# Graph network kernel, message pass: gates behind gelus, update gelu out of PSUM, half of the second normalisation on ScalarE, tick order changed; start terms loaded three batches ahead

## The reference, cut to what matters

```
h = relu(layernorm(x)); x = x + attention(h)           # layer 0
h = relu(layernorm(x)); x = x + layer1(h)              # layer 1, the "message pass"
h = relu(layernorm(x)); x = x + propagate(h)           # layer 2, 16 rounds
h = relu(layernorm(x)); x = x + gcn(h)                 # layer 3

# layer 1
edge_input = concat(h[src], edge_attr)                 # 96 + 32 features
messages   = gelu(edge_input @ mW1 + mb1) @ mW2 + mb2
gates      = sigmoid(gelu(edge_input @ gW1 + gb1) @ gW2 + gb2)
aggregated = segment_sum(messages * gates, dst)
update     = gelu(concat(h, aggregated) @ uW1 + ub1) @ uW2 + ub2
y          = h + update
layer1     = (y - mean) * rsqrt(var + 1e-5) * ln_g + ln_b
```

## Time and profile before

| | |
|---|---|
| median of 3 runs | 11957.47 us (11951.58 to 11964.21) |
| profiled execution | 11956.96 us |
| its span | 11955.2 us |
| PE busy | 6883.6 us, 58% |
| DVE busy | 6471.5 us, 54% |
| ACT busy | 4318.2 us, 36% |
| POOL busy | 8488.0 us, 71% |
| mean granted TensorE clock | 0.738 of 2.4 GHz |

### The profile page before, as it was taken

The page is one execution under the profiler, slowest core; times in us unless marked ns, Lnnn a source line. Parts: engine busy times, 40 slices in busy tenths (PEclk is TensorE's granted clock), DMA queues, the critical chain, the costliest instruction groups (busy, mean ns, idle before and its releaser), DMA issues. The chain is left out here.

```text
span 11955.2 us, 140496 instructions
## 1 busy us (share of the span) xinstructions
PE 6883.6 (58%) x20977; PEld 4313.5 (36%) x20977; DVE 6471.5 (54%) x24207; ACT 4318.2 (36%) x14541; POOL 8488.0 (71%) x8647
## 2 busy tenths in 40 slices
PE   4687677975655556556565565555556555672000
PEld 4566566664433323323333332333323323352000
DVE  6577896898844444444444444444444444575444
ACT  5698566877722222222222222222222222373000
POOL 6675765536777777777777777777777777776777
PEclk7665667877777777777777777777777777896555
DMA  7998885668854444444444444444444444473221
GB/s 246 304 251 239 267 276 150 188 182 271 259 152 140 118 115 116 114 114 117 113 118 114 114 116 114 118 113 114 118 114 117 113 115 118 150 233 123 64 66 55
DMA packets 1059890, 1804.54 MB, mean 151 GB/s; under 512 B 515278, under 2 KB 525948, under 8 KB 1059661
## 3 DMA queue, kind: packets, MB, share of 16 engines
q1 hardware_dynamic: 777325, 1384.14, 34.9%
q0 software_dynamic: 282336, 418.19, 16.1%
HBM read 1070.12 MB, written 738.89 MB: 151 GB/s over the span
## 5 line engine op out<-in xcount | busy, mean ns | idle before, releaser
L351 POOL DMA_INDIRECT r_g<-y_t,idx_s x5768 | 5545.6, 961 | 1984.6 <-issue 1856.9
L1895 DVE SCALAR_TENSOR_TENSOR F<-r_g,scan_s,F 128x96 f32<-128x96 f32 x5488 | 1769.4, 322 | 3981.9 <-DMA r_g<-y_t,idx_s 3088.0
L1995 PE MATMUL r_pu<-r_S,ident 128*128 128x384 f32 x2688 | 1734.2, 792 | 2803.7 <-DVE r_S L1897 2803.7
L2023 ACT ACTIVATE H<-r_pu,kc_e 128x96 f32 (+1 forms) x5474 | 1340.3, 355 | 5542.5 <-PE r_pu L1995 5508.8
L1995 PEld LDWEIGHTS r_pu<-r_S,ident 128*128 128x128 f32 x2688 | 678.5, 278 | 3553.5 <-DVE r_S L1897 3219.8
L1897 DVE SCALAR_TENSOR_TENSOR r_S<-r_S,scan_s,r_g 128x96 f32<-128x96 f32 x5488 | 1716.3, 313 | 0.0
L1977 PE MATMUL r_pu<-H,ident 128*128 (+2 forms) x2744 | 1530.5, 649 | 93.4 <-DMA r_c<-c_t 87.8
L1978 PE MATMUL r_pu<-r_c,ident 128*128 128x384 f32 (+1 forms) x2744 | 1347.3, 579 | 0.0
L1977 PEld LDWEIGHTS r_pu<-H,ident 128*128 128x128 f32 x2744 | 776.4, 284 | 766.8 <-issue 656.9
L1978 PEld LDWEIGHTS r_pu<-r_c,ident 128*128 128x128 f32 x2744 | 666.8, 243 | 560.9 <-issue 361.9
L2282 PE MATMUL e_pc<-e_S,B 128*128 128x96 f32 x2 | 0.7, 474 | 1050.9 <-DVE e_o L2326 1050.9
(11 more groups left out here) (329 smaller groups left out, 12095.3 us busy)
## 6 DMA issues: line engine op xcount, KB each, us to landing
r_c<-c_t SPq DMA_DIRECT2D x686, 384.0 KB
y_t<-H SPq DMA_DIRECT2D x672, 384.0 KB
r_g<-y_t,idx_s POOLq DMA_INDIRECT x5880, 2.5
kv_t<-n_kv SPq DMA_DIRECT2D x49, 776.0 KB, 6.7
y_t<-d_yx SPq DMA_DIRECT2D x98, 384.0 KB
agg_t<-e_S SPq DMA_DIRECT2D x49, 416.0 KB, 4.5
x1s_t<-e_xb SPq DMA_DIRECT2D x50, 384.0 KB, 4.9
h_t<-e_h SPq DMA_DIRECT2D x50, 384.0 KB, 5.3
```

What stands on the lines that cost most here:

```text
L351: G.indirect_dma_start(out=to(j), out_offset=None, in_=table, in_offset=bass.IndirectOffsetOnAxis(ap=idx_s[:, h, j:j + 1], axis=0)).then_i ...
L1895: own.add(V.scalar_tensor_tensor(out=F[:, 0:D], in0=g[:, j, :], scalar=scan_s[:, h, j, 1:2], in1=F[:, 0:D], op0=ALU.mult, op1=ALU.add))
L1995: last = T.matmul(pu[h % 2][g][:], ident[:], S[:, h % 2, 4 * g:4 * g + 4, :], start=False, stop=True)
L2023: last = A.activation(v[:, j, :], pu[h % 2][j // 4][:, j % 4, :], ACT.Copy, scale=k[:, j, 0:1])
```

## The change

In the message pass:

- The update's gelu is no longer applied in SBUF. TensorE turns the hidden values as they are, and ScalarE's copy out of PSUM becomes the gelu.
- Of the second normalisation, columns 4 to 7 stay on VectorE (`scale2`, in two operations over 384 elements). Columns 0 to 3 are done on ScalarE (`norm2`, four Relu activations with scale and bias); VectorE prepares their bias by one small product. SyncE's store waits for both.
- Both tanh of a tick stand together, first in ScalarE's tick, then both roots, then all gelus.
- The order in a tick and some lags change on all engines but GpSimd.

In the rounds c has four tiles instead of two and is loaded three batches ahead instead of one, and so is H in the first round. To make room, some tiles (`dst_i`, most weights) are freed before the rounds.

```diff
-        def gelu(b, n, h):
-            after(act, s_pr, b + 1)
-            A.activation(ur[:, h % 2], ur[:, h % 2], ACT.Gelu).then_inc(s_gr, 1)
...
-                A.copy(uT[0:D, h % 2, g, :], pu[0:D, :]).then_inc(s_ut, 1)
+                A.activation(uT[0:D, h % 2, g, :], pu[0:D, :], ACT.Gelu).then_inc(s_ut, 1)
...
+        def norm2(b, n, h):                                    # ScalarE
+            act.wait_ge(s_st[h], 32 * n)
+            after(act, s_rn2, b + 1)
+            for j in range(HALF):
+                last = A.activation(yx[:, h, j, 0:D], yx[:, h, j, D:2 * D], ACT.Relu,
+                                    scale=rn2[:, h, 0, j:j + 1], bias=rn2[:, h, 1, j:j + 1])
+            last.then_inc(s_yn, 1)
...
-        def norm2(b, n, h):                                    # VectorE
+        def scale2(b, n, h):
             own6.step(b)
             after(dve, s_mv2, b + 1)
             dve.wait_ge(s_st[h], 32 * n)
-            own6.add(V.tensor_tensor(yx[:, h, :, 0:D], yx[:, h, :, D:2 * D],
-                                     mv2[:, h, :, 0:1].to_broadcast([P, J, D]), ALU.subtract))
+            after(dve, s_yn, b - 3)
+            v = yx[:, h, HALF:J, 0:D]
+            own6.add(V.tensor_tensor(v, yx[:, h, HALF:J, D:2 * D],
+                                     mv2[:, h, HALF:J, 0:1].to_broadcast([P, J - HALF, D]), ALU.subtract))
...
+            V.scalar_tensor_tensor(out=rn2[:, h, 1, 0:HALF], in0=mv2[:, h, 0:HALF, 0], scalar=-1.0,
+                                   in1=rn2[:, h, 0, 0:HALF], op0=ALU.mult, op1=ALU.mult).then_inc(s_rn2, 1)
...
         def store(b, n, h):                                    # SyncE
             after(sp, s_y0, b + 1)
+            after(sp, s_yn, b + 1)
...
-        skewed(sp, (6, load_u), (16, store), (0, edges_only(load)), (9, load_h1), (11, load_xb),
-               (7, edges_only(store_sums)), total=NX)
+        skewed(sp, (6, load_u), (14, store), (0, edges_only(load)), (9, load_h1), (10, load_xb),
+               (8, edges_only(store_sums)), total=NX)
...
-        skewed(pe, (3, hidden_m(0)), (7, turn_gelu(0)), (3, hidden_g(0)), (3, hidden_m(1)),
-               (3, hidden_g(1)), (4, edges_only(message(1))), (2, edges_only(turn(0))),
-               (4, edges_only(message(0))), (2, edges_only(turn(1))), (8, outer_layer(1)),
-               (7, turn_gelu(1)), (8, outer_layer(0)), (6, edges_only(carry)), total=NX)
+        skewed(pe, (8, outer_layer(0)), (3, hidden_g(0)), (7, turn_hidden(0)), (3, hidden_m(0)),
+               (8, outer_layer(1)), (4, edges_only(message(1))), (3, hidden_g(1)),
+               (2, edges_only(turn(0))), (7, turn_hidden(1)), (3, hidden_m(1)), (2, edges_only(turn(1))),
+               (4, edges_only(message(0))), (6, edges_only(carry)), total=NX)
...
-        skewed(dve, (10, scale), (11, update), (6, hidden), (9, add(1)), (9, add(0)), (9, stats),
-               (5, gated(1)), (12, norm2), (5, gated(0)), (11, stats2), (5, total), total=NX)
+        skewed(dve, (7, hidden), (9, add(0)), (10, scale), (12, scale2), (6, total), (11, stats2),
+               (9, add(1)), (9, stats), (10, update), (5, gated(1)), (5, gated(0)), total=NX)
...
# the rounds
-                            after(sp, s_up, r * NB + b - 1)
+                            after(sp, s_up, r * NB + b - 3)
                             sp.sem_inc(s_turn_s)
-                            sp.dma_start(cs[:, h % 2], slots_of(c_t, 0, b)).then_inc(s_c[h % 2], 16)
+                            sp.dma_start(cs[:, h], slots_of(c_t, 0, b)).then_inc(s_c[h], 16)
...
-                        skewed(sp, (1, store), (-1, load))
+                        skewed(sp, (1, store), (-3, load))
```

More of the change, by code:

```diff
@@ L17 @@
 K = 4
+HALF = J // 2
 OF = [len(range(h, NB, K)) for h in range(K)]
@@ L273, in program, with weight @@
         weight_loads = []
-        def weight(name, parts, width, rows=D + 1):
-            t = sb(name, [rows, width])
+        def weight(name, parts, width, rows=D + 1, ctx=None):
+            t = sb(name, [rows, width], ctx=ctx or nodes)
             for r0, r1, c0, c1, a in parts:
@@ L285, in col @@
             return v.rearrange("(n a) -> n a", a=1)
+        w_3 = weight("w_3", [(0, D, 0, D, W3)], D, D, outer)
+        r_rows = weight("r_rows", [(0, 1, 0, D, row(ln_g)), (0, 1, D, 2 * D, row(ln_b)),
+                                   (0, 1, 2 * D, 3 * D, row(b3))], 3 * D, 1, outer)
+        r_all = sb("r_all", [P, 3, D])
+        nodes = outer.enter_context(ExitStack())
+        dst_i = sb("dst_i", [P, CH], I32, nodes)
         w_kvq = weight("w_kvq", [(0, D, 0, D, Wk), (0, D, D, 2 * D, Wv), (0, D, 2 * D, 3 * D, Wq),
@@ L301, in program @@
         c_u1 = weight("c_u1", [(0, D, 0, 1, col(ub1))], 1, D)
[L302 to L306, removed]
+        w_mu = sb("w_mu", [D + 1, D], F32, nodes)
         iroot = sb("iroot", [P, CHS], F32, nodes)
@@ L1409, in carry, with turn_hidden @@
                             T.matmul(pm[:, 0:D], B[:], S[:, h, J - 1, :], start=True, stop=True).then_inc(s_cr, 1)
-                    def turn_gelu(g):
+                    def turn_hidden(g):
                         def run(b, n, h):
-                            after(pe, s_gr, b + 1)
+                            after(pe, s_pr, b + 1)
                             after(pe, s_ut, 2 * b + g)
@@ L1492, in norm @@
                         ln_norm(act, b, hs[:, h % 2], ln[:, h % 2], rn[:, h], s_rn, ACT.Identity).then_inc(s_ln, 1)
[L1494 to L1497, removed]
+                    def norm2(b, n, h):
[5 more added lines that the diff above has]
+                        last.then_inc(s_yn, 1)
+                    skewed(act, (5, tanh(1)), (5, tanh(0)),
                            (11, lambda b, n, h: ln_root(act, b, mv2[:, h], rn2[:, h], s_mv2, s_sd2)),
-                           (7, gelu_turned(1)), (2, edges_only(turned(1))), total=NX)
+                           (9, lambda b, n, h: ln_root(act, b, mv[:, h], rn[:, h], s_mv, s_sd)), (3, gelu_g(0)),
+                           (7, gelu_u(0)), (3, gelu_m(0)), (9, norm), (2, edges_only(turned(0))), (3, gelu_g(1)),
+                           (-2, edges_only(slots)), (7, gelu_u(1)), (4, edges_only(masks)), (3, gelu_m(1)),
+                           (2, edges_only(turned(1))), (12, norm2), total=NX)
                 @block.vector
@@ L1598, in norm2 @@
                         own6.end()
-                        V.scalar_tensor_tensor(out=yx[:, h, :, 0:D], in0=yx[:, h, :, 0:D], scalar=0.0,
-                                               in1=rn2[:, h, 0, :].unsqueeze(2).to_broadcast([P, J, D]),
+                        V.scalar_tensor_tensor(out=rn2[:, h, 1, 0:HALF], in0=mv2[:, h, 0:HALF, 0], scalar=-1.0,
+                                               in1=rn2[:, h, 0, 0:HALF], op0=ALU.mult, op1=ALU.mult).then_inc(s_rn2, 1)
+                        V.scalar_tensor_tensor(out=v, in0=v, scalar=0.0,
+                                               in1=rn2[:, h, 0, HALF:J].unsqueeze(2).to_broadcast([P, J - HALF, D]),
                                                op0=ALU.max, op1=ALU.mult).then_inc(s_y0, 1)
-                    skewed(dve, (10, scale), (11, update), (6, hidden), (9, add(1)), (9, add(0)), (9, stats),
-                           (5, gated(1)), (12, norm2), (5, gated(0)), (11, stats2), (5, total), total=NX)
+                    skewed(dve, (7, hidden), (9, add(0)), (10, scale), (12, scale2), (6, total), (11, stats2),
+                           (9, add(1)), (9, stats), (10, update), (5, gated(1)), (5, gated(0)), total=NX)
                     dve.wait_ge(s_y0, NX)
+                    dve.wait_ge(s_yn, NX)
                     first.add(V.tensor_copy(zx[:, 0:2 * D], yx[:, NB % K, 0, :]))
@@ L1977, in start @@
                                 T.matmul(to, ident[:], cols(H, b)[:, c, :], start=True, stop=False)
-                                T.matmul(to, ident[:], cs[:, h % 2, c, :], start=False, stop=False)
+                                T.matmul(to, ident[:], cs[:, h, c, :], start=False, stop=False)
                         def add(b, n, h):
```

17 lines of the change are left out of this document (8 added, 9 removed).

## The result

The changed kernel takes 12013.34 us (median of 5 runs, 11999.72 to 12015.95), the kernel before beside it 11952.9 (5 runs, 11936.65 to 11964.21): ratio 1.0052, interval [1.0040, 1.0064]. It is slower by some 60 us. Forecast: 11997, range 11930 to 12060. The profiled execution has a span of 12011.3 us, against 11955.2: +56.1.

A forecast was written before the change was run, and what follows sets the result against it. VectorE was taken to pace the message pass at 15.0 us a tick, gathers the rounds; a new ring through SyncE's store gives 35 x 1.4 = 49 us, other ticks -9, rounds zero: 11957 + 40 = 11997 us, range 11930 to 12060.

The forecast's parts named there:

- The ring: Message pass: ScalarE's norm to Relus, SyncE's store to h1 load, landing, VectorE, closing once per tick; 11.8 us plus landing.
- The landing: Message pass, h1 load behind two 384 KB stores: 4.6 us from issue to landing, where the median was 3.5.
- The tick: Message pass: 16.4 us a tick in the changed kernel, ends 14.9 and 18.1, against 15.0 before.
- SyncE's part: Message pass, SyncE's queue: two stores, then edge load to h1 load, 3.3 us of the ring.
- rival 1: Message pass: the ring closes but the h1 load's landing stays 3.5 us; tick 15.3, +1 us, 11958; chance 0.20.
- Rival 4: Message pass: h1 load runs only when stores are through, landing 5.2, tick 17.0, +61 us, 12018; chance 0.13.
- full ring ticks: Message pass, ticks 14 to 48, where stores and edge loads both run: 35 ticks x 1.4 us = 49 us.
- The light ticks: Message pass, ten full ticks beside the ring's (9 to 13, 49 to 53): -9 us.
- Rival 2: Message pass: the ring has unseen slack, VectorE stays the bound; tick 13.8, -54 us, 11903; chance 0.13.
- The split of the second norm: Message pass, VectorE: two operations halved to 384 elements, one small product added; net -0.6 us a tick.
- The rounds: Fourteen middle rounds: start-term loads three batches ahead change nothing, since gathers pace a round at 502.6 us; zero.
- Rival 3: Message pass: TensorE's clock falls to 0.62, its work of 17.9 us becomes the tick; +93 us, 12050; chance 0.12.

The follow-up runs named there:

- f3: Changed kernel with the message pass's store moved in SyncE's tick from ahead of the edge load to behind the h1 and xb loads: 11888.37 us, 0.9954 of before.
- g4: Changed kernel with ScalarE's four Relus moved from its tick's end to right ahead of the first norm, SyncE's order kept: 11926.0 us, 0.9949 of before.
- g3: Changed kernel with the second norm wholly on VectorE again, so the store waits for VectorE alone: 11956.11 us, 0.9975 of before.
- g1: Changed kernel with two rows of the second norm on ScalarE instead of four (HALF = 2): 12016.38 us, 1.0023 of before.
- g2: Changed kernel with SyncE's edge load moved behind the h1 and xb loads, the store still ahead of them: 11992.42 us, 1.0005 of before.
- f1: The changed kernel again, no edit: 12011.34 us beside 11944.65 for the kernel before, 1.0056.
- f2: The kernel before again, no edit, one profiled run: 11968.16 us.
- f4: Kernel before with only the rounds' part of the change (four start-term tiles loaded three batches ahead, SBUF moves): 11942.97 us, 1.0001 of before.

## Why the prediction was right, and where it wasn't

**The mechanism: right.** The ring ScalarE, SyncE, landing, VectorE was forecast with its links in order; the turn of 16.65 us has these and no other. It was cut or shortened at five places, and the tick fell each time: at SyncE's order (f3), at ScalarE's order (g4), at the wait (g3), at its Relus (g1), at the edge load (g2). The landing changed only along with g2, and VectorE's 0.96 us was not touched.

**The tick: right by luck, since two errors cancel.** Forecast 16.4, measured 16.65 in that turn. ScalarE 7.2 against 7.1, VectorE 0.95 against 0.96. SyncE's part was forecast as 3.3 and is 4.9: I took the edge load's issue from a tick in which no stores stood ahead of it; right behind two stores of 384 KB its second transfer takes 1.56 us to issue (1.35 in the tick before), and its third 0.7. The landing was forecast as 4.6 and is 3.3 with its hand-over (median 3.6), as rival 1 had it. When the load gets out at 2324.15, the DMA engines' rate has fallen to 145 GB/s in that microsecond, from 286 and 244 in the two before, so the stores are mostly through. Rival 4 (5.2, strictly behind the stores) is wrong here. In g2, where the load goes out 1.39 us behind the first store, the rival's way of counting (the stores hold the engines for 5 us) gives 3.5 + 3.6 = 7.1, and the median is 5.1, so about half of it holds.

**The cost of the full ring ticks: nearly right.** By the norms, here of the kernel before,

```profile
2031.66 2.62 ACT L340 ACTIVATE e_ln<-e_h,e_rn 128x96 f32<-128x96 f32 x7
...
2573.39 2.97 ACT L340 ACTIVATE e_ln<-e_h,e_rn 128x96 f32<-128x96 f32 x8
```

the 4th to the 40th batch; in the changed kernel the 4th and the 39th:

```profile
2009.46 2.97 ACT L341 ACTIVATE e_ln<-e_h,e_rn 128x96 f32<-128x96 f32 x8 [1.11 <-DVE e_rn L334]
...
2595.13 2.97 ACT L341 ACTIVATE e_ln<-e_h,e_rn 128x96 f32<-128x96 f32 x8 [4.46 <-DVE e_rn L334]
```

35 ticks take 585.7 us, 16.7 each; before, 36 ticks took 541.7, 15.05 each (the first 35 of them 529.0, 15.1 each). The 35 ticks cost 585.7 - 529.0 = 57 us, where I had 35 x 1.4 = 49. The trace of f1 repeats the 585.7 (585.8), and two more traces of the kernel before's message pass (f2, f4) have 529.8 and 527.0.

**The light ticks: wrong in sign at the end.** I counted -9 us for the ticks without a full ring. The pass does begin sooner: add(0) or add(1) first runs at 1961.7, 10.6 us before the 1972.26 of the earlier trace rows. But the ring goes on when the edge loads have ended, since the stores still run: the h1 load then goes out 1.14 us behind the store, the add follows 6.0 us or more behind it, and the norms still start every 15.3 to 15.8 us for four ticks. And the last batch has a new wait that the prediction did not list:

```profile
2706.94 0.40 SPq L1344 DMA_DIRECT2D agg_t<-e_S  x1
```

```profile
2713.00 0.94 POOL L1370 DMA_INDIRECT Z<-agg_t,idx_f  x1 [120.02 <-DMA agg_t<-e_S]
```

```profile
2715.52 0.26 DVE L1547 TENSOR_TENSOR e_S<-Z,e_pm 128x96 f32<-128x96 f32 x1 [15.35 <-DMA Z<-agg_t,idx_f]
```

These are timelines of SyncE, GpSimd and VectorE. The last store of the sums goes out at 2706.94, GpSimd's single gather Z waits for it, and VectorE waits 15.35 us for the gather. The last row of the last batch's sums had started at 2689.3:

```profile
L1534 DVE SCALAR_TENSOR_TENSOR e_S<-e_S,scan_s,e_g x392: 308/319/385, 1928.3 to 2689.3; 128x96 f32<-128x96 f32 x196
```

Before, the last such row starts at 2642.9 and the store follows at 2643.3:

```profile
L1342 SPq DMA_DIRECT2D agg_t<-e_S x49: 343/361/623, 1937.0 to 2643.3; - x49
```

The store of the sums stands behind the x2s store in SyncE's tick, so it too waits for ScalarE's Relus. I followed the h1 load behind the blocked store and not the sums store behind both. The Relus are not all of it: in g3, whose store doesn't wait for ScalarE, VectorE still waits 5.19 us for this gather, and in g4, whose Relus are early, 10.60. The change also moved the sums store one tick later (lag 8, not 7), and no run has that apart.

```profile
2622.53 0.26 DVE L1538 TENSOR_TENSOR e_S<-Z,e_pm 128x96 f32<-128x96 f32 x1 [5.19 <-DMA Z<-agg_t,idx_f]
```

The sum over the traces, from rows: the first norm is 15.5 us earlier (1973.27 against 1988.78, given by the timelines of ScalarE) and the 4th 22.2 us; in the 35 ticks that follow 585.7 against 529.0, +56.7; from the 39th norm to the 50th 162.5 against 133.0, +29.4, the 15.35 among them; from there to the first gather of the rounds -0.3, over the rounds -8.9, behind them +1.4. -22.2 + 56.7 + 29.4 - 0.3 - 8.9 + 1.4 = +56.1, the difference of the spans. The light ticks at both ends are -22.2 + 29.4 = +7, where I had -9. That is the 16 us between forecast and median; the ring's 8 us more (56.7 against 49) and the 8 us less behind the pass (-0.3 - 8.9 + 1.4) cancel. The two ends are not equally firm: f1 repeats the changed kernel's 162.5 us at the end as 163.1, but the 4th norm of the kernel before stands at 2031.66, 2021.61 and 2033.55 in three traces (before, f2, f4), so the -22.2 is good to some 10 us only. The rounds' -8.9 can't be told from nothing: f4's ratio for the rounds' part is 1.0001, with an interval of 11 us to either side.

**VectorE's own tick, and the rivals.** Rival 2's tick of 13.8 us, VectorE-bound, is what f3 (13.77) and g4 (13.85) show; only its condition was missing. The reading of the kernel before, VectorE at 14.1 us a tick and 0.9 of small waits, was right in kind. VectorE's waits for others there, 2000 to 2600 us (us in total, times, longest), and then its longest ones in g3, 2050 to 2600 us, where it has the same operations:

```profile
DVE e_rn L332 <- ACT e_rn L327: 15.4, 20, 2.2
...
DVE e_ur L1549 <- PE e_pu L1416: 4.9, 4, 1.4
...
DVE e_ur L1549 <- issue: 2.9, 3, 1.3
DVE e_h L1557 <- PE e_pv L1425: 2.3, 8, 0.3
```

```profile
DVE e_mv L323 <- DVE e_st L318: 11.7, 72, 0.5
DVE e_st L318 <- DVE e_h L1555: 3.9, 15, 0.3
```

The first four are 25.5 us in 40 ticks, 0.6 us a tick. In g3 VectorE waits for no other engine, only for its own operations, and its tick is 15.16 - 14.49 = 0.67 us shorter. So VectorE's tick without waits for others is 14.5 us in the mean, not the 14.1 of the one tick that I read, and the rest of the change (the order, the gelu out of PSUM, one table load fewer; no run has them apart) takes those waits away. Rival 2's 13.8 was 13.5 with 0.3 of waits; the runs have 13.8 with none. The split of the second norm is worth 0.64 to 0.72 us (g4, f3), where I had 0.6.

**The rest.** The rounds were costed at nothing, and f4 bears it out. One part of their working doesn't hold: the 5768 gathers of the earlier trace rows leave out each round's last eight, which have a line of their own, and the pass before the rounds is longer than a round (2734 to 3292 us, 558), so that 7530.2/15 = 502.0 agrees by chance. The 14 rounds alone, 3292 to 10325 us, say the same more directly:

```profile
L351 POOL DMA_INDIRECT r_g<-y_t,idx_s x5376 | 5130.3, 954 | 1778.3 <-issue 1740.4 <-ACT scan_s L2009 23.2 <-DVE r_S L1897 14.6
L1958 POOL DMA_INDIRECT r_g<-y_t,idx_s x112 | 106.9, 955 | 34.1 <-issue 34.1
```

Gathers and gaps fill all of these 7033 us. Rival 3 is out: the granted clock is 0.82 against 0.83, and ScalarE doesn't wait for TensorE's transposes (1.0 us at L1457 in the 600). TensorE's new order was costed at nothing, but no run has it alone; with the ring open the granted clock is 0.88 in 2000 to 2400 us (f3, g4; 0.83 in the kernel before). The table loads are two a tick, as forecast.

## What to carry to other kernels

When a store gets a second engine to wait for, look up what is queued behind it, all of it, and ask whether that work leads back to the same engine within one tick; if so, add up the turn. A closed turn costs also where every engine on it is idle a quarter of the time, and it opens at any link: here the place of one step in the queue's order was worth 1% (12011.34 to 11888.37 us, f1 and f3). An issue time read behind an empty queue is not that behind a large transfer, and issuing a load sooner gives part of the time back in its landing.

## What the runs showed of the hardware

How long a transfer takes to issue depends on what stands just ahead of it in SyncE's queue. The second edge transfer (L242) takes 0.4 to 0.6 us in f3, but for one at 1.45, and 1.26 to 1.67 us in the changed kernel's 35 ticks where it comes right behind two stores of 384 KB. This isn't particular to small pieces: in f3 the store of the sums comes right behind those stores, and its issue has a median of 2.39 us, against 0.37 in the changed kernel. A load issued 1.4 us after the first of the two stores lands in 5.1 us, issued 4.9 us after it in 3.6 (medians of g2 and of the changed kernel).

```profile
L1344 SPq DMA_DIRECT2D agg_t<-e_S x49: 363/2388/3129, 1952.6 to 2597.1; - x49
```

One chip ran the kernel before in 14110 us, in all other comparisons it took 11945 to 11987, with register moves of 688 ns instead of 29 on SyncE; there an edit that is worth nothing elsewhere was worth 0.6%. A ratio from one chip can be that chip's.
